# Reordering the score tiles, the bases and the row maxima in three exact-softmax attention layers

## The reference, cut to what matters

```
q = (x @ w_q).reshape(T, 16, 64) / 8        # T = 2048, 16 heads
k = (x @ w_k).reshape(T, 16, 64) / 8
v = (x @ w_v).reshape(T, 16, 64)
dot = einsum('qhd,khd->hqk', q, k)          # float32 scores
dot = where(k <= q, dot, -inf)              # the causal layer only
att = softmax(dot, axis=-1)
out = einsum('hqk,khd->qhd', att, v).reshape(T, 1024) @ w_u + b_u
x = x + out
```

## Time and profile before

| | us |
|---|---|
| median of three runs | 3922.62 (3916.49 to 3926.24) |
| the profiled execution, its own time | 3927.83 |
| its span, first to last instruction | 3925.9 |

### The profile page before, as it was taken

The page is one execution under the profiler, slowest core; times in us unless marked ns, Lnnn a source line. Parts: engine busy times, 40 slices in busy tenths (PEclk is TensorE's granted clock), DMA queues, the critical chain, the costliest instruction groups (busy, mean ns, idle before and its releaser), DMA issues.

```text
span 3925.9 us, 67314 instructions
## 1 busy us (share of the span) xinstructions
PE 3653.8 (93%) x25781; PEld 1931.0 (49%) x25781; DVE 2896.5 (74%) x5821; ACT 2270.9 (58%) x2635; POOL 11.1 (0%) x17
## 2 busy tenths in 40 slices
PE   4999999999999958999999995699999999999997
PEld 2445445454554425555555554245545455554544
DVE  5777878778787676777777765477777877778784
ACT  3666666666666515655655652466666666666663
POOL 1000000000000000000000000000000000000000
PEclk9999999999999979999999997899999999999998
DMA  1000000000000000000000000000000000000000
GB/s 51 7 9 10 9 12 7 9 10 9 9 8 8 8 13 7 15 15 12 15 12 13 11 15 3 19 7 12 8 9 10 10 9 10 9 10 8 7 9 17
DMA packets 44405, 44.40 MB, mean 11 GB/s; under 512 B 16466, under 2 KB 30554, under 8 KB 43834
## 3 DMA queue, kind: packets, MB, share of 16 engines
q1 hardware_dynamic: 44090, 40.09, 3.4%
HBM read 37.56 MB, written 1.70 MB: 10 GB/s over the span
## 4 chain that ended last, share of the span: by engine, by line
PE 79%; DVE 11%; issue 5%; ACT 4%; DMA 1%; SPq 1%; DVEq 0%; ACTq 0%
PE ps L558 75%; DVE over L1231 2%; DVE acc L1211 2%; DVE wexp L1231 1%; DVE x L1369 1%; ACT Kh L986 1%; ACT work L1014 1%; PE ps L877 1%; PE ps L888 1%; DVE Kd L1154 1%; PE ps L547 1%; DVE stats L1123 1%; PE ps L917 0%; SPq L468 0%; SPq L436 0%
## 5 line engine op out<-in xcount | busy, mean ns | idle before, releaser
L1014 ACT ACTIVATE work<-ps 128x1024 f32<-128x1024 f32 (+1 forms) x1344 | 1277.0, 995 | 957.2 <-PE ps L558 953.0
L1211 DVE TENSOR_TENSOR acc<-acc,work 128x1024 f32<-128x1024 f32 (+2 forms) x1152 | 1352.0, 1174 | 47.3 <-ACT work L1014 11.5
L558 PE MATMUL ps<-work,V 128*64 128x512 f32 (+3 forms) x5376 | 1234.8, 579 | 0.0
L558 PEld LDWEIGHTS ps<-work,V 128*64 128x64 f32 x5376 | 450.7, 137 | 539.5 <-issue 444.2
L558 PE MATMUL ps<-Qh,Kh 64*128 64x512 f32 (+3 forms) x2688 | 652.9, 481 | 26.1 <-issue 10.6
L1231 DVE CUSTOM_DVE_ANT_0 over<-ps,over,mpart 128x512 f32<-128x512 f32 (+3 forms) x642 | 422.6, 696 | 309.3 <-PE ps L558 309.2
L558 PE MATMUL ps<-Qh,Kl 64*128 64x512 f32 (+3 forms) x2688 | 526.0, 385 | 0.0
L558 PE MATMUL ps<-Ql,Kh 64*128 64x512 f32 (+3 forms) x2688 | 522.6, 383 | 0.0
L558 PE MATMUL ps<-auxQ,auxK 64*128 64x512 bf16 (+3 forms) x2688 | 518.5, 380 | 0.0
L1231 DVE CUSTOM_DVE_ANT_0 wexp<-ps,wexp 128x512 f32<-128x512 f32 (+1 forms) x632 | 377.0, 636 | 29.8 <-PE ps L558 29.8
L558 PE MATMUL ps<-Kh,Qh 64*128 64x512 f32 (+2 forms) x1520 | 350.7, 467 | 34.1 <-DVE mpart L1231 13.0
(11 more groups left out here) (187 smaller groups left out, 2541.3 us busy)
## 6 DMA issues: line engine op xcount, KB each, us to landing
rden<-inverse_sums SPq DMA_DIRECT2D x192, 128.0 KB, 2.9
auxQ<-mrow SPq DMA_DIRECT2D x384, 1.0 KB
wqk<-in_wqk SPq DMA_DIRECT2D x24, 128.0 KB, 2.4
dcomp<-rden SPq DMA_DIRECT2D x192, 2.0 KB
wv<-in_wv SPq DMA_DIRECT2D x24, 64.0 KB, 2.2
inverse_sums<-rcomp SPq DMA_DIRECT2D x96, 4.0 KB, 1.3
work<-in_mlp_w SPq DMA_DIRECT2D x1, 1024.0 KB
work<-in_c_aux SPq DMA_DIRECT2D x1, 1024.0 KB, 4.9
```

Source lines behind the costliest of these rows:

```text
L558: return pe.matmul(o, w, m, start=start, stop=stop, skip_group_check=True)
L1014: act.activation(work[:, 2 * e:2 * e + 2, q0:CH], ps[:, b:b + 2, q0:CH], ACT.Exp, scale=L.scale).then_inc(s["p_ready"], 1)
L1211: dve.tensor_tensor(o, o, work[:, slots[two]:slots[two] + 2, q0:CH], ALU.add).then_inc(s["acc_ready"], 1)
```

## The change

In the causal layer the second base (slot 1) is issued behind the third score tile and no longer ahead of it. On DVE, in all three layers, the order at the head of a cycle becomes: maxima of slot 0, maximum of tile 0 if any, maxima of slot 1, and only then the last addition of the cycle before. Nothing is added or removed: each engine's instructions are the same in number and shape, and so are the waits.

```diff
@@ row_block, TensorE
+                    base_last = m0 is not None or L.causal
+                    if base_last:
                         pe.wait_ge(s["p_ready"], tiles + 1)
                         scores(n, p, 2 * g + 1, 0)
                     if 1 in pending:
                         m, u = pending[1]
                         at_least(pe, s["top_ready"], L.NTOP * m + L.tops_to[u])
                         base(m, m % 2, u)
-                    if m0 is None:
+                    if not base_last:
                         pe.wait_ge(s["p_ready"], tiles + 1)
                         scores(n, p, 2 * g + 1, 0)
@@ cycle, VectorE
                     for sl, m, u in before_:
-                        if sl == 0:
-                            tops(m, u)
+                        if sl == 1 and L.tile0_in(x) is not None:
+                            tops(m, 0)
+                        tops(m, u, slot=sl)
                     for which in last:
                         add(*which)
-                    if L.tile0_in(x) is not None:
-                        tops(L.tile0_in(x), 0)
-                    for sl, m, u in before_:
-                        if sl == 1:
-                            tops(m, u, slot=1)
                     for m, c in L.due(L.mul_at, x):
                         normalise(m, c)
```

## The result

The changed kernel takes 4052.33 us (median of five runs, 4049.3 to 4060.16) against 3922.62: slower by 130 us, ratio 1.0328 with a 95% interval of 1.0315 to 1.0342. The forecast was 4026 in a range of 3978 to 4064. The profiled span went from 3925.9 to 4050.6 us.

The account below looks back on a forecast made before the run. PE's program order was taken to bound the kernel. The op jobs (35), mt jobs (22) and causal layer (46) summed to +103 us on the median of 3922.62, giving 4026 us, range 3978 to 4064.

Parts of the forecast that it names:

- Bound by PE's order: Whole kernel: PE's program order sets the time, any wait of PE is paid; PE busy 93% of the span.
- The 0.78 on DVE: Layers with G = 16: DVE waits for the second base, so everything behind the slot-1 maxima comes 0.78 us later.
- What the sooner release gives: Layers with G = 16: slot-1 maxima start 0.36 us sooner, but the second excess still waits for exponentials; counted 0.
- op jobs, forecast 35: Layers with G = 16: PE waits 0.58 us for the delayed normalise, 60 jobs; 35 us, bounds 30 to 42.
- mt jobs, forecast 22: Layers with G = 16: later DVE work delays the maxima rows' DMAs and next chunk's scores; 22 us, bounds 10 to 35.
- den jobs, forecast 0: Layers with G = 16: the chunk's last addition ends at 677.17, just before PE needs it; if not hidden, 6 us.
- The causal layer, forecast 46: Causal layer: seven cycle kinds lose 0.9 to 1.1 us, three gain 0.17 to 0.36; +46 us, bounds 32 to 56.
- The sign given for this layer: Causal layer: PE's waits for mpart/mcol up by 40 to 50 us, its busy share down from 94.5% to about 89%.
- The change works: Rival: PE's 56 us of waits for maxima shrink by 31 us at best, to 3892; chance 0.03.
- Nothing measurable: Rival: gain and loss cancel as PE's added idle time replaces idle time a little later; 3923, chance 0.03.
- the rivals in which only one kind of layer pays: Only the causal layer loses, 3959 to 3969, or only the layers with G = 16, 3980; together chance 0.12.
- this rival: Causal layer: PE's clock falls in one or two more cycles of each pair, 14 or 27 us; 4040 to 4053, chance 0.12.

Follow-up runs that it names:

- mt ahead: The changed kernel, but in the layers with G = 16 DVE's part of the mt job stands ahead of its cycle's first addition; 4018.29 us.
- both repairs: The changed kernel with normalise ahead of the last addition and, in layers with G = 16, DVE's part of mt ahead of the first; 3981.32 us.

## Why the prediction held, and where its terms were off

**Bound by PE's order.** Right: of the 125 us by which the span grew, PE is busy in 14 and idle in 111. The sum of +103 came out at +130 by the medians, so the measured 4052 lies 26 us above the point of the forecast and 12 below the end of its range. The missing part is named below: 20.5 us at the mt jobs, 5.6 at the op jobs and 1 in the causal layer, less 2 in the other cycles; the rest is the difference between medians and the two profiles.

**The 0.78 on DVE.** Right. `normalise` starts 698.95 - 695.93 = 3.02 us behind the second base, where it was 676.31 - 674.09 = 2.22: 0.80 later.

**What the sooner release gives.** Counted as 0, and it is: in these layers the slot-0 excess starts 0.16 to 0.35 us sooner in most cycles, and the next cycle does not. The eight cycles without a delayed consumer sum to -0.6 and -1.6 us.

**op jobs, forecast 35.** Right in mechanism, 40.6 measured. The term was 0.58 a job; it measured 0.6 to 0.8. The forecast let PE start 0.05 after `oN`; in the timeline it starts 699.79 - 699.64 = 0.15 after, which over 60 jobs is the missing 6 us.

**mt jobs, forecast 22, and den jobs, forecast 0.** This is the term that was mis-sized: 42.5 together. Two steps made it so. First, `mval` moved by more than 0.51 us: by 0.72 in the cycle shown (g = 11), by 0.62 to 0.86 in the others and by 0.98 where the maximum of tile 0 is. The last addition and the first of the next step now stand side by side and the second needs the first's result, so that DVE takes 2.55 us for the two and `mval` starts 710.73 - 708.26 = 2.47 behind the first. The 0.51 comes out only if both take the 1.14 from start to start that one took before (675.09 - 673.95). Second, "PE would wait for the slot-0 maxima there anyway" did not hold for g = 3 and 7: the first scores came 0.8 to 0.9 us later, only a third of it was absorbed at g = 4, and none to speak of at g = 8. (The K and Q projections that the forecast names stand in slot 1 in these layers, not in slot 2.) The cases with the maximum of tile 0, at g = 12 of the third layer, were the dearest with 0.93 each, and were put at 0.5; only that layer has them, not both. The bounds of the term, 10 to 35, were too narrow; the range held because the other bounds had room.

The den job, put at nothing, was in fact hidden in the changed kernel: PE's waits for an addition sum to 0.3 us in one place. That the first scores of the same cycles were late had moved PE behind it. With mt ahead this cover is gone and the wait shows:

```profile
PE ps L558 <- DVE acc L1213: 2.9, 13, 0.5
```

That is half of the 6 us that did not come back with mt ahead (36.7 of 42.5); the other half was not traced further.

**The causal layer, forecast 46.** 46.8 measured. By the forecast's kinds, in nearly all pairs that have units and where the clock did not differ: seven at +0.7 to +1.2 a cycle (one of them, g = 3 of the first pair, at +1.5) and three at -0.1 to -0.3. For g = 3 the excess was worked out at +1.11 and measured at +1.11. That the total is met to 1 us is in part luck: without the clock it would be 48, and the seven kinds alone gave 52 where 51 was put. The base alone costs 12 us more (+59.2). About 8 of that is the clock, which fell in eight cycles against three; the rest is mostly that the three good kinds give nothing without DVE's new order. The sign given for this layer was met in part: PE's waits for `mpart` and `mcol` in it rose by 33 us (31.3 to 64.5) and not by 40 to 50, since 8 more stand under `work`, and its busy share fell to 91.1% and not to 89%.

**The rivals.** "The change works" was right about its own part, with PE's waits for the maxima down by 9 us where the base stayed, and wrong about the slack behind it. "Nothing measurable" and the rivals in which only one kind of layer pays fall by the table: 80.9 us in the two layers with G = 16 and 46.8 in the causal one. The clock did not fall more often in the changed kernel's profile (three cycles of the causal layer against four), so this rival did not decide; it moved the experiments by several us, both ways.

The Trainium skill ("DMA: Bandwidth & Descriptors", the two cost components) gives about 2.0 us of fixed cost per DMA, and fits it on DMAs that GpSimd issues, not SyncE as here. An estimate from it, counted from the end of SP's issue as in the prediction, would put the first scores 2.55 + 2.0 = 4.6 us after SP's first issue; counted from the start of the last of the four issues, of 0.57 each, 1.98 + 2.0 = 4.0. They came after 3.60, below both.

## What to carry to other kernels

An addition that stands between two dependent steps of an in-order queue may be their cover: moving it away gave a release 0.36 us sooner, that nobody was waiting for, and made everything behind it 0.8 later, that two consumers were waiting for, with a third behind them. Before reordering a queue, list who waits for each instruction behind the moved one and how much slack each has; in this kernel it was 0.0 to 0.2 us. And a cost removed in one place may uncover the next: repairing mt showed the wait for den.

The causal base stood where PE had to wait for an exponential anyway. Moved behind the tile that ends this wait it came 1.03 us later at g = 3 (2042.87 - 2039.48 = 3.39 into the cycle in place of 1973.63 - 1971.27 = 2.36), and with one score tile left to cover its maxima in place of two, PE idled 0.20 + 0.71 us that it had not idled before.

## What the hardware showed that was not expected

- Two additions on DVE, the second reading what the first writes, took 2.55 us for the two where one takes 1.22: 0.1 between them. An addition behind the maxima starts 0.08 before they end: 697.82, together with the READ_ACCUMULATOR of 0.08 that ends them.
- PE's clock in the causal layer fell at the same place of the cycle order in pair after pair: at g = 9 in four of the eight pairs before, at g = 5 in seven with both repairs. Each fall made that cycle 1.5 to 1.7 us longer. Windows of the run with the causal order alone, and of the one with the base alone, clock behind POOL:

```profile
1514.00:2342.00 828.00, 796.13 (x7114) 467.68 (x7112) 608.64 (x1454) 495.33 (x616) 0.00 (x0) 1.00 0.04 13
```

```profile
1513.00:2413.00 900.00, 815.03 (x7110) 472.25 (x7110) 607.13 (x1453) 504.65 (x616) 0.00 (x0) 0.98 0.04 12
```

The first has no fall (nor has the run with DVE's order everywhere), and about half of its gain in the causal layer is that; the second has eight. Why one order of the same instructions keeps the clock and the other does not was not tried.
